# Preparing the channel-mix stage inside the last cross-attention head of a decoder layer

## What is computed

```python
x = x + self_attention(layernorm(x))             # 16 heads, causal, relative bias
x = x + cross_attention(layernorm(x), context)   # 8 heads of 128; all 2048 queries see all 4096 context rows
y = layernorm(x)                                 # over the 256 channels
y_prev = y shifted by one token within its batch (zero ahead of the first)
xr = mu_r * y + (1 - mu_r) * y_prev              # token shift
xk = mu_k * y + (1 - mu_k) * y_prev
out = x + sigmoid(xr @ W_r.T) * (square(relu(xk @ W_k.T)) @ W_v.T)
```

## Time and profile before

| | |
|---|---|
| median of three runs | 2679.68 us |
| profiled execution: its own time | 2684.01 us |
| its span | 2682.1 us (1.9 us lie around it) |
| PE busy | 2571.0 us (96%) |
| DVE busy | 1926.2 us (72%) |
| ACT busy | 1617.8 us (60%) |
| POOL busy | 129.4 us (5%) |
| mean granted TensorE clock | 0.982 |

### The profile page before, as it was taken

One profiled execution on the slowest core, in us unless ns is written; L12 is line 12 of the kernel. 1 busy time (PEld: TensorE's weight loads), 2 busy tenths in 40 slices (PEclk: granted clock), 3 DMA queues, 4 the chain that ended last, 5 costly groups with the idle time before them and its releaser, 6 DMA issues. The chain is left out here.

```text
span 2682.1 us, 47140 instructions
## 1 busy us (share of the span) xinstructions
PE 2571.0 (96%) x17680; PEld 2316.2 (86%) x17680; DVE 1926.2 (72%) x3637; ACT 1617.8 (60%) x3064; POOL 129.4 (5%) x159
## 2 busy tenths in 40 slices
PE   7799979999999999999999999999999999999976
PEld 5699868998899889988999899989998899889975
DVE  5588867776777677777777777767776777677765
ACT  5599845566565656664656466556565665566655
POOL 1353010000000000000000000000000000000003
PEclk8899989999999999999999999999999999999998
DMA  6896342001200110012000300030002000210000
GB/s 198 225 188 148 84 166 79 17 16 64 71 17 16 64 63 25 16 43 85 17 24 10 117 17 16 16 110 25 16 16 107 28 16 16 79 46 20 9 12 32
DMA packets 93773, 156.53 MB, mean 58 GB/s; under 512 B 42496, under 2 KB 56000, under 8 KB 93600
## 3 DMA queue, kind: packets, MB, share of 16 engines
q1 hardware_dynamic: 89600, 141.20, 17.5%
q0 software_dynamic: 3248, 12.72, 1.5%
q10 hardware_dynamic: 752, 0.26, 0.0%
HBM read 122.56 MB, written 27.39 MB: 56 GB/s over the span
## 5 line engine op out<-in xcount | busy, mean ns | idle before, releaser
L1485 ACT CAST pt_hi<-xt_ps 128x512 fp32r<-128x512 f32 x1024 | 593.3, 586 | 573.2 <-PE xt_ps L1455 557.5
L1551 DVE TENSOR_TENSOR pt_lo<-xt_ps,pt_hi 128x512 fp32r<-128x512 f32 x1024 | 704.8, 688 | 266.1 <-ACT pt_hi L1485 262.8
L1540 DVE TENSOR_SCALAR_CACHE_REDUCE xprobs<-xs_ps 128x1024 f32<-128x1024 f32 x512 | 626.7, 1224 | 174.3 <-PE xs_ps L1404 169.4
L1466 PE MATMUL xo_ps<-pt_hi,v_hi 128*128 128x256 f32 x2048 | 649.5, 317 | 1.3 <-DVE pt_lo L1551 1.3
L1491 ACT ACTIVATE xprobs<-xprobs,xneg_max 128x1024 f32<-128x1024 f32 x512 | 592.2, 1157 | 26.7 <-DVE xneg_max L1546 26.7
L1455 PE MATMUL xt_ps<-ident,xprobs 128*128 128x128 f32 x4096 | 604.2, 272 | 0.0
L1466 PE MATMUL xo_ps<-pt_lo,v_hi 128*128 128x256 f32 x2048 | 577.6, 282 | 0.0
L1466 PE MATMUL xo_ps<-pt_hi,v_lo 128*128 128x256 f32 x2048 | 576.0, 281 | 0.0
L1455 PEld LDWEIGHTS xt_ps<-ident,xprobs 128*128 128x128 f32 x4096 | 485.0, 140 | 60.7 <-issue 6.9
L1466 PEld LDWEIGHTS xo_ps<-pt_hi,v_hi 128*128 128x128 f32 x2048 | 388.8, 190 | 4.0 <-DVE pt_lo L1551 1.3
L1466 PEld LDWEIGHTS xo_ps<-pt_lo,v_hi 128*128 128x128 f32 x2048 | 389.4, 190 | 1.9
(11 more groups left out here) (210 smaller groups left out, 2764.3 us busy)
## 6 DMA issues: line engine op xcount, KB each, us to landing
v_split<-ctx_split SPq DMA_DIRECT2D x68, 768.0 KB, 5.8
xq<-x_split SPq DMA_DIRECT2D x64, 512.0 KB, 3.3
q_st<-rel_split SPq DMA_DIRECT2D x32, 256.0 KB, 4.3
q_st<-q_split SPq DMA_DIRECT2D x32, 192.0 KB, 4.4
k_st<-k_split SPq DMA_DIRECT2D x32, 192.0 KB, 4.7
ctx_split<-ctx_out POOLq DMA_DIRECT2D x8, 768.0 KB, 4.4
q_split<-stage_hi SPq DMA_DIRECT2D x8, 512.0 KB, 5.0
k_split<-stage_hi SPq DMA_DIRECT2D x8, 512.0 KB, 5.0
```

The costliest lines, as they stand in the source:

```text
L1466: last = pe.matmul(o_ps[:, 0:GQ], v[:, vs], pt[:, c % 3, GQ * j:GQ * (j + 1)], start=c == 0 and j == 0 and m == 0, stop=c == PIECES - 1 an ...
L1485: act.copy(pt_hi[:, c % 3, :], t_ps[:, c % 3, :]).then_inc(t_rounded, 1)
L1540: dve.tensor_scalar(probs[:, par if kind == "A" else 1 - par, t, CHUNK * i:CHUNK * (i + 1)], s_ps[:, buf, :], LOGIT, None, ALU.mult, ALU.m ...
L1551: dve.tensor_tensor(pt_lo[:, c % 3, :], t_ps[:, c % 3, :], pt_hi[:, c % 3, :].bitcast(F32), ALU.subtract).then_inc(t_ready, 1)
```

## The change

The preparation of the channel mix is put into items of the last head. `ChannelMix` is made before `cross_attention` and holds the stage's tensors in rows that exist already: the split weights and their raw parts in space of `v_split`, `kv_raw`, `v_rest`, `wq_raw` and `bout`; the normalised rows `y` and the mixed rows in one half of the probability tile, relu, square and gates in the other; the rounded and rest parts of batch b in the key or value row b (`k_hi`, `k_lo`, `v_hi`, `v_lo`). Small per-token values lie in `wo_raw`.

- SP, in the last head, after its query loads: six weight loads of 128 x 256 and the two mu loads.
- `LAST_6` (the step before `LAST_7`, new): DVE takes moments of tiles 0 to 7, one a piece, pieces 4 to 11.
- `LAST_7`: moments of tiles 8 to 11; at pieces 3, 5, 7 one weight each is rounded on ACT (2 copies) and split on DVE (2 subtractions); at 13 DVE makes nu and the variances of tiles 0 to 11, at 14 ACT takes their root, at 15 DVE makes the scales.
- `LAST_8`: ACT normalises tiles 0 to 3 at pieces 0 to 3; DVE takes moments of 12 and 13 at 5; PE transposes batch 0 at 5 (`MT`, 8 transposes into `xs_ps`, a chunk of its own); ACT scales at 6 to 9, DVE adds the earlier token at 8 to 11, ACT rounds at 10 to 13, DVE takes the rests for k at 12 and 14.
- POOL, once its waits (all pieces before `LAST_8` transposed, scales ready) are met: normalises tiles 4 to 11 (8 `tensor_scalar` instructions), then takes the rests for r of batch 0.
- `channel_mix` then starts with the transposes of batch 1 and the keys of batch 0, with no wait but the block's; the moments of tiles 14 and 15, their variances, root and scales, and the normalising of tiles 12 to 15 are left in it. `act_hi` and `act_lo` hold two batches in place of four, so their rounding waits for matmuls two batches back.

```diff
+MIX_6 = {4 + i: [("mom", i)] for i in range(8)}
+MIX_7 = {1: [("mom", 8)], 2: [("mom", 9)], 3: [("mw", 0)], 5: [("mw", 1)], 7: [("mw", 2)], 11: [("mom", 10)], 12: [("mom", 11)],
+         13: [("var",)], 14: [("root",)], 15: [("scale",)]}
+MIX_8 = merged({t: [("norm", t)] for t in range(4)}, {5: [("mom", 12), ("mom", 13), ("MT", 0)]},
+               {6 + i: [("own", i // 2, 1 - i % 2)] for i in range(4)}, {8 + i: [("earlier", i // 2, 1 - i % 2)] for i in range(4)},
+               {10 + i: [("round", i // 2, 1 - i % 2)] for i in range(4)}, {12: [("rest", 0)], 14: [("rest", 1)]})
+LAST_6 = with_pieces(merged(SCORES, EXPS, AHEAD, OUT, MIX_6), [("O",)])
+LAST_7 = with_pieces(merged(SCORES, EXPS, OUT, MIX_7), [("O",)])
+LAST_8 = with_pieces(merged({1: [("I",)], 4: [("out",)]}, MIX_8), [("O",)])
...
+    def round_weights(self, act, n):
+        act.wait_ge(self.loaded, 128)
+        for h in range(CH):
+            act.copy(self.w_hi[:, n, h, :], self.w_raw[n][h]).then_inc(self.w_hi_ready, 1)
...
+    def take_root(self, act, tiles, number):
+        cols = slice(tiles.start, tiles.stop)
+        act.wait_ge(self.var_ready, number)
+        act.activation(self.root[:, cols], self.var_eps[:, cols], ACT.Sqrt).then_inc(self.root_ready, 1)
...
+    def scale_own(self, act, m, n, turned):
+        act.activation(self.whole(m, n), turned, ACT.Identity, scale=self.mu[:, m, n % CH:n % CH + 1]).then_inc(self.parted, 1)
+
+    def add_earlier(self, dve, m, n, turned):
+        dve.wait_ge(self.parted, 2 * n + 2)
...
+    def rest_of_mixed(self, eng, m, n, done):
+        eng.wait_ge(self.mix_rounded, 2 * n + 2 - m)
...
+            pool.wait_ge(turned, (XH * G - 1) * PIECES)
+            pool.wait_ge(mix.rstd_ready, 1)
+            for t in AHEAD_TILES[QI:]:
+                pool.tensor_scalar(mix.y[:, t, :], x[:, t, :], mix.mv[:, t, 0:1], mix.rstd[:, t:t + 1],
+                                   ALU.subtract, ALU.mult).then_inc(mix.y_pool, 1)
+            for h in range(CH):
+                mix.rest_of_mixed(pool, 0, h, mix.r_rest)
...
+            def turn_first(buf):
+                pe.wait_ge(mix.y_ready, QI)
+                for h in range(CH):
+                    for t in range(QI):
+                        last = pe.transpose(s_ps[:, buf, N * h + P * t:N * h + P * (t + 1)], mix.y[:, t, P * h:P * (h + 1)], ident[:])
+                return last
...
+            for t in LAST_TILES[2:]:
+                mix.moments(chain, t)
+            mix.variances(chain, LAST_TILES)
             for b in range(B + 1):
...
+                if b + 1 < B:
+                    for h in range(CH):
+                        add_earlier(CH * (b + 1) + h)
+                if b == 0:
+                    mix.scales(chain, LAST_TILES, 2)
...
-            for n in range(2 * CH):
+            for n in range(CH, 2 * CH):
                 turn(n)
-            pe.wait_ge(w_ready, 3)
```

More of the change, by code:

```diff
@@ L1129 @@
+AHEAD_TILES, LAST_TILES = range(0, 3 * QI), range(3 * QI, NT)
 PIECES = KEYS // (2 * P)
-IS_CHUNK = ("A", "A+", "out", "Q+", "K+", "V+", "V")
+IS_CHUNK = ("A", "A+", "out", "Q+", "K+", "V+", "V", "MT")
 def with_pieces(extra, ahead=()):
@@ L1219, in head @@
         for g in range(2 + 2 * LOOPED, G - 1):
-            step(STEP, g, STEP_AT[g])
+            step(LAST_6 if last else STEP, g, STEP_AT[g])
         if last:
@@ L1334, in head @@
                     load_queries(group)
+                if last:
+                    mix.load_weights(sp)
                 if not last:
@@ L1530, in _ @@
         def _(dve):
+            chain = Chain(dve, mix.dve_self)
             def run(items, h, g, s, par, chunk, chunk_par):
@@ L1614, in run @@
                         dve.tensor_tensor(wo_lo[:], wo_raw[:], wo_hi[:].bitcast(F32), ALU.subtract).then_inc(wo_w, 1)
+                    elif kind == "mom":
+                        dve.wait_ge(freed, chunk + n)
+                        mix.moments(chain, item[1])
+                    elif kind == "mw":
+                        mix.rest_of_weights(dve, item[1])
+                    elif kind == "var":
+                        dve.wait_ge(mix.loaded, 128)
+                        chain(dve.tensor_scalar(mix.nu[:], mix.mu[:], -1.0, 1.0, ALU.mult, ALU.add))
+                        mix.variances(chain, AHEAD_TILES)
+                    elif kind == "scale":
+                        mix.scales(chain, AHEAD_TILES, 1)
+                    elif kind == "earlier":
+                        mix.add_earlier(dve, item[2], item[1], s_ps[:, 1 - buf, N * item[1]:N * (item[1] + 1)])
+                    elif kind == "rest":
+                        mix.rest_of_mixed(dve, 1, item[1], (freed, mix.k_rest)[item[1]])
                     n += kind in IS_CHUNK
@@ L1618, in _, with channel_mix @@
             dve.wait_ge(freed, ALL_CHUNKS)
-def channel_mix(nc, a, x, ident, out):
+            dve.wait_ge(mix.k_rest, 1)
+            chain.wait()
+            mix.chained = chain.n
+def channel_mix(nc, x, ident, out, mix):
     with ExitStack() as ctx:
@@ L1628, in sem @@
             return ctx.enter_context(nc.semaphore(name))
[L1630 to L1641, removed]
+        act_hi, act_lo = sb("act_hi", [P, 2, CH, N], F32R), sb("act_lo", [P, 2, CH, N], F32R)
+        relu, square = mix.late[:, 0:2, :], mix.late[:, 2:4, :]
+        gate = mix.late[:, 4:6, :].rearrange("p z (u c) -> p (z u) c", c=C)
+        gated = mix.late[:, 6:8, :].rearrange("p z (u c) -> p (z u) c", c=C)
+        w_hi, w_lo = mix.w_hi, mix.w_lo
         y_ps = ctx.enter_context(nc.psum_tensor("mix_y", [P, 2, N], F32))
@@ L1691, in add @@
                 pool.tensor_tensor(x[:, t, :], x[:, t, :], gated[:, t % 4, :], ALU.add).then_inc(added, 1)
-            for b in range(B):
+            for b in range(1, B):
                 for h in range(CH):
[L1695 to L1698, removed]
+                    mix.rest_of_mixed(pool, 0, CH * b + h, mix.r_rest)
+                for t in range(QI * (b - 1), QI * b):
+                    add(t)
@@ L1700, in _ @@
         @block.vector
         def _(dve):
[L1702 to L1723, removed]
-                for m in (1, 0):
[L1725 to L1734, removed]
+            chain = Chain(dve, mix.dve_self, mix.chained)
+            def add_earlier(n):
+                for m in (1, 0):
+                    mix.add_earlier(dve, m, n, y_ps[:, n % 2, :])
@@ L1880, in gates_and_values @@
                 b = t // QI
[L1881 removed]
+                pe.wait_ge(mix.r_rest, CH * (b + 1))
                 pe.wait_ge(act_ready, CH * (b + 1))
@@ L1884, in gates_and_values @@
                     pe.wait_ge(gated_ready, t - 3)
-                rows = slice(P * t, P * (t + 1))
-                for c0, w, hi, lo in ((0, 0, mix_hi[:, 0], mix_lo[:, 0]), (C, 2, act_hi, act_lo)):
-                    passes = [(zs, ws, h) for h in range(CH) for zs, ws in ((hi, w_hi), (hi, w_lo), (lo, w_hi))]
+                rows = slice(P * (t % QI), P * (t % QI + 1))
+                gate_parts = [[mix.part(b, part, 0, h) for h in range(CH)] for part in range(2)]
+                value_parts = [[kept[:, b % 2, h, :] for h in range(CH)] for kept in (act_hi, act_lo)]
+                for c0, w, (hi, lo) in ((0, 0, gate_parts), (C, 2, value_parts)):
+                    passes = [(zs[h], ws, h) for h in range(CH) for zs, ws in ((hi, w_hi), (hi, w_lo), (lo, w_hi))]
                     for i, (zs, ws, h) in enumerate(passes):
-                        last = pe.matmul(rv_ps[:, t % 4, c0:c0 + C], zs[:, h, rows], ws[:, w, h, :],
+                        last = pe.matmul(rv_ps[:, t % 4, c0:c0 + C], zs[:, rows], ws[:, w, h, :],
                                          start=i == 0, stop=i == len(passes) - 1)
                 last.then_inc(rv_done, 1)
-            for n in range(2 * CH):
+            for n in range(CH, 2 * CH):
                 turn(n)
-            pe.wait_ge(w_ready, 3)
             for b in range(B + 1):
```

235 lines of the change are left out of this document (135 added, 100 removed).

## The result

The changed kernel takes 2657.25 us (median of 4 runs, 2656.0 to 2659.8) against 2678.41 us (4 runs) before: ratio 0.9922, 95% interval 0.9909 to 0.9934, or 20.9 us less (17.7 to 24.4).

A forecast was written before the change was run, and what follows sets the result against it. The prediction took a chain of small preparations on SP, DVE and ACT, 21.1 us before the first key matmul, as the bound. -19.95 + 1.3 + 0.9 + 0.3 = -17.45 us off 2679.68 gave 2662.2 us, range 2658.8 to 2667.5.

The forecast's parts named there:

- Start of the stage: Channel mix start: DVE, not PE, sets batch 1's keys, which start at 12.1 us, 19.95 us sooner.
- Root, 1.3: End of `LAST_7`: ACT's table load and root lie on the path to the last value matmuls; cost 1.3 us.
- rival 2: Table load in `LAST_7`: a switch drains as well, ACT stands 1.4 us longer; -16.1 us, 2663.6 us; chance 0.07.
- MT, 0.9: `LAST_8`: 8 added transposes on PE, which is the bound there; cost 0.9 us.
- 0.3 for the late last `pt_lo`: `LAST_8`, piece 14: DVE's rest holds back the last `pt_lo`, where no slack is; 0.3 us, upper bound 1.7.
- DVE and POOL in `LAST_8`: `LAST_8`: DVE's additions exceed the period by 0.45 us in all, absorbed by slack; POOL's rests might slow DVE's.
- Rival 1: `LAST_8`: cover too thin, full queues gain nothing from overlap; 4 us more, -13.5 us, 2666.2 us; chance 0.22.
- POOL's normalising: POOL during `LAST_8`: 8 instructions of 128x256 at 0.75 to 1.5 us each, hidden; cost nothing.
- Rival 4: Block's end: POOL's normalising and rests hold it; slower than before from 4.5 us an instruction; chance 0.04.
- From there on ... I cost that part at nothing: Channel mix from batch 1's keys to the end: engines keep the order and counts of before; cost nothing.
- Rival 3: More gained: load starts under the copy, `MT` falls into a PE wait, shorter chain; -19.5 us, 2660.2 us; chance 0.09.

## Why the prediction was off

Step by step, in its own order:

- **Start of the stage.** "The keys of batch 1 start at 12.1, 19.95 us sooner": measured 12.05 after the first transpose and 20.06 sooner. Its reason, DVE and not PE, is shown by the moved scales. Right, the clock of the first keys included.
- **Root, 1.3:** measured 1.26 for step 63, 1.09 of it given back when the load moved. Right in place and size; PE waited 0.82 us on the last `pt_lo`, where about 0.9 was forecast. The Trainium skill (ScalarE: Activation LUTs, "What ACT_TABLE_LOAD costs") would have it 1.4 more, for a drain; in the changed kernel and in the one with the root moved, the load starts 0.02 to 0.03 us behind the cast's end (2565.48 and 2569.91) and the root 0.01 us behind the load. The measurement decides: no drain showed, and rival 2 falls.
- **MT, 0.9, and 0.3 for the late last `pt_lo`:** step 64 grew by 0.89 in all, and from the first transpose of `MT` to the next one of a piece are 0.87. The 0.3 was not there as an addition. The last head cost 2.15, not 2.5.
- **DVE and POOL in `LAST_8`.** DVE ran without a gap, as costed, and POOL's rests (1.29 each, at 2584.52 and 2586.82) did not fall on DVE's: those two kept 0.68 and 0.69, the second with 0.1 us of overlap. Where the two engines' rests do meet, behind the block's start, DVE's takes 1.42 (at 2604.32), as in the rows of before. Rival 1 falls in the changed kernel: PE had no wait over 0.3 us in pieces 1 to 14.

```profile
2584.87 0.74 DVE L1228 SCALAR_TENSOR_TENSOR xprobs<-xs_ps,nu,xprobs 128x511 f32<-128x511 f32 x1
2585.53 0.68 DVE L1704 TENSOR_TENSOR pt_lo<-xt_ps,pt_hi 128x512 fp32r<-128x512 f32 x1
2586.13 0.68 DVE L1237 TENSOR_TENSOR k_hi<-xprobs,k_hi 128x512 fp32r<-128x512 f32 x1
2586.73 1.36 DVE L1704 TENSOR_TENSOR pt_lo<-xt_ps,pt_hi 128x512 fp32r<-128x512 f32 x2
2588.01 0.69 DVE L1237 TENSOR_TENSOR k_hi<-xprobs,k_hi 128x512 fp32r<-128x512 f32 x1
```

At the old addresses step 64 took 21.79 us, 0.7 more, in one profile. That is the clock: behind two waits of PE at the end of step 63 (0.84 and 0.82) it was at half speed from about 2580.9 to 2584.3, and from there on the step runs 0.65 us behind that of the changed kernel. The changed kernel has nearly the same two waits (0.87 and 0.82) and kept the full clock. The stretch and the first 12 transposes at the old addresses, then the same transposes in the changed kernel:

```profile
2581.00:2584.00 3.00, 3.00 (x16) 2.84 (x15) 1.51 (x5) 2.02 (x5) 2.42 (x2) 0.50 0.00 0
...
2581.26 2.76 PE L1595 MATMUL xt_ps<-ident,xprobs 128*128 128x128 f32 x12
```

```profile
2569.07 1.47 PE L1595 MATMUL xt_ps<-ident,xprobs 128*128 128x128 f32 x12
```

- **POOL's normalising:** 1.22 us an instruction, inside the 0.75 to 1.5 given, hidden. Rival 4 needed 4.5.
- **"From there on ... I cost that part at nothing":** it cost 1.72 between these two profiles, 1.2 of it in keys and transposes at a lower clock, 0.6 in slower `mix_rv` matmuls. A term of the sum, mis-sized.
- **The step that failed** is one that the prediction took without a word: that the steps with unchanged items, O 1 to O 62, would keep their time. Its sum has no term for them. The new tiles `mu` and `nu` shift `pt_hi` and all behind it by 64 bytes, and that is worth 5.5 us: the run with the 64 bytes alone has the gain, and the change at the old addresses has lost it. There the change took 2663.04 us, inside the range. The terms that were there sum to -16.2 by what they measured (-20.06 + 1.26 + 0.89 + 1.72), against -17.45 forecast; with -5.5 it is -21.7. A little of the distance in the time itself is chance: before ran at 2678.41 beside the change, 1.27 below the 2679.68 that the forecast started from. The range moved by as much would begin at 2657.5, still above the 2657.25. Rival 3 (-19.5) had the size nearly, for other reasons, none of which the runs bear out.

## What to carry to other kernels

A stage whose engines wait on small preparations is worth as much as its bare chain, if the stage ahead has slack between neighbours on each engine; cost each insert as a step (start to start) against the period, and keep table loads behind the last instruction that another engine waits for (here 1.09 us of one step, too little to show in the whole time). When a change adds or moves an SBUF tile, compare the address of every operand of the bounding engine, and measure the old work at the new addresses: here it was a quarter of the gain. To find such a term, lay a ruler of equal events over both traces rather than compare spans.

## What the hardware showed that I had not expected

Sixty-four bytes ahead of `pt_hi`, with the same instructions, changed the pace of PE's matmuls at full clock: value matmuls (128x256) 282 to 278 ns, score matmuls (128x512) 390 to 395. Seven placements gave 2075.3 to 2086.2 us for the same 61 steps; kernels of different work with these tiles at the same places mod 256 agreed within 0.15 us. In the wait of 6.64 us ahead of batch 1's keys PE's clock fell near 2601.8 and came back near 2612, 6.2 us into the keys; before, in the wait of 5.30 us, it fell near 2631.4 and was back 3.6 us into them.
